# Softplus's logarithm as a degree-9 polynomial in the sigmoid, and one scan over all batches of a piece

## The reference

```python
# layer 0
a = xw_t + prev_h @ Wh
i, f, o = sigmoid(a[:, :H]), sigmoid(a[:, H:2*H]), sigmoid(a[:, 2*H:3*H])
g = tanh(a[:, 3*H:])
c = f * c + i * g ;  h = o * tanh(c)
x = x + hs
# layer 1
conv = conv_b + sum(x_pad[:, k:k+L, :] * conv_w[k, 0] for k in range(K))   # K = 8
proj = conv @ Wp + bp
B_t, C_t = softplus(proj[..., :N]), tanh(proj[..., N:])                    # N = 64
u = x @ Ws + bs
decay = 1 - softplus(dt_log) * softplus(A_log)
state = decay * state + softplus(dt_log) * B_t * u_t ;  y_t = C_t * state
x = x + y @ Wo + bo
```

## Time and profile before

| | before |
|---|---|
| median of 3 runs | 1922.39 us (1920.68 to 1922.65) |
| the profiled execution's own time | 1919.75 us |
| its span | 1917.8 us |
| granted TensorE clock, mean | 0.995 |
| busy: TensorE matmul, VectorE, ScalarE, GpSimd | 94%, 72%, 53%, 18% |

### The profile page before, as it was taken

The page is one execution under the profiler, slowest core; times in us unless marked ns, Lnnn a source line. Parts: engine busy times, 40 slices in busy tenths (PEclk is TensorE's granted clock), DMA queues, the critical chain, the costliest instruction groups (busy, mean ns, idle before and its releaser), DMA issues.

```text
span 1917.8 us, 123272 instructions
## 1 busy us (share of the span) xinstructions
PE 1810.3 (94%) x52690; PEld 1419.5 (74%) x52690; DVE 1388.6 (72%) x6911; ACT 1015.9 (53%) x4057; POOL 337.5 (18%) x1544
## 2 busy tenths in 40 slices
PE   5888999999999999999999999999999999999976
PEld 3666777777777777777777777777777777777865
DVE  8677667777677776777777677777777777867675
ACT  5555455555555555555555545555555555545442
POOL 1111111111111111111111111111111111111110
PEclk9999999999999999999999999999999999999998
DMA  6111111111111211111111111111111121211100
GB/s 236 53 42 38 48 54 37 51 55 44 53 51 39 63 43 54 44 50 55 48 57 40 54 54 42 59 45 51 53 53 45 46 56 40 74 38 50 46 15 24
DMA packets 112668, 100.81 MB, mean 53 GB/s; under 512 B 20353, under 2 KB 86453, under 8 KB 111094
## 3 DMA queue, kind: packets, MB, share of 16 engines
q1 hardware_dynamic: 111704, 90.79, 15.6%
q10 hardware_dynamic: 416, 2.13, 0.3%
HBM read 50.90 MB, written 41.94 MB: 48 GB/s over the span
## 4 chain that ended last, share of the span: by engine, by line
PE 78%; DVE 10%; ACT 5%; issue 3%; POOL 2%; DMA 1%; SPq 0%; ACTq 0%; POOLq 0%; DVEq 0%
PE recA L540 28%; PE recB L534 24%; PE pw L501 12%; PE pbc L585 10%; DVE tr L900 4%; ACT act L783 3%; POOL h L468 2%; DVE hz L931 2%; DVE pre L906 2%; DVE prod L914 1%; ACT tc L793 1%; PE pw L485 1%; PE po L605 1%; PE pu L558 1%; DMA wpk<-in_L_cond_Wh_dram 1%
## 5 line engine op out<-in xcount | busy, mean ns | idle before, releaser
L783 ACT ACTIVATE act<-pre 128x64 f32<-128x64 f32 x1024 | 262.7, 257 | 854.3 <-DVE pre L909 838.1
L540 PE MATMUL recA<-whi,hz 128*16 128x256 f16 x8176 | 516.0, 275 | 75.6 <-DVE hz L931 62.3
L534 PE MATMUL recB<-whi,hz 128*32 128x128 f16 x16352 | 577.6, 219 | 0.4 <-issue 0.4
L534 PE MATMUL recB<-wlo,hz 128*32 128x128 f16 x16352 | 577.6, 219 | 0.1
L540 PE MATMUL recA<-wlo,hz 128*16 128x256 f16 x8176 | 512.6, 273 | 0.0
L534 PEld LDWEIGHTS recB<-whi,hz 128*32 128x32 f16 x16352 | 438.0, 97 | 10.2 <-issue 0.6
L534 PEld LDWEIGHTS recB<-wlo,hz 128*32 128x32 f16 x16352 | 437.9, 97 | 2.6 <-issue 0.2
L540 PEld LDWEIGHTS recA<-whi,hz 128*16 128x16 f16 x8176 | 199.9, 88 | 303.5 <-DVE hz L931 281.6
L900 DVE STREAM_TRANSPOSE tr<-recA 128x256 f32<-128x256 f32 x512 | 230.0, 449 | 203.5 <-PE recA L540 201.6
L585 PE MATMUL pbc<-yt,wpk 128*128 128x256 f32 (+5 forms) x1120 | 329.6, 400 | 0.0
L468 POOL TENSOR_TENSOR h<-osc,tc 128x16 f32<-128x16 f32 x1024 | 226.3, 221 | 465.4 <-ACT tc L793 465.4
(11 more groups left out here) (157 smaller groups left out, 1989.8 us busy)
## 6 DMA issues: line engine op xcount, KB each, us to landing
xw_rows<-xs SPq DMA_DIRECT2D x128, 256.0 KB, 2.5
seed<-xw_rows SPq DMA_DIRECT2D x1008, 32.0 KB, 2.0
xn<-in_x_dram SPq DMA_DIRECT2D x32, 256.0 KB
out_dram<-ot SPq DMA_DIRECT2D x32, 256.0 KB, 3.0
seed<-in_L_cond_Wh_dram ACTq DMA_DIRECT2D x2, 1024.0 KB, 6.6
wpk<-in_L_cond_Wh_dram SPq DMA_DIRECT2D x2, 1024.0 KB, 12.2
wlo<-in_L_cond_Wx_dram SPq DMA_DIRECT2D x2, 1024.0 KB, 13.7
xs<-in_L_cond_Wx_dram SPq DMA_DIRECT2D x1, 1024.0 KB, 10.0
```

The lines of the kernel that those rows point to most:

```text
L534: ins = pe.matmul(rec[1][32 * j:32 * j + 32, 0:128], h[:, k, 2 * NB * (1 - c):2 * NB * (1 - c) + 32], w[:, k, 4 * (2 + c) + j, :], start=F ...
L540: ins = pe.matmul(rec[0][32 * j:32 * j + 2 * NB, 0:256].rearrange("p (c f) -> p c f", c=2), h[:, k, 2 * NB:4 * NB], w[:, k, :, :].rearrang ...
L783: act_eng.activation(act[q][:, 0:G, :].rearrange("p g n -> p (g n)"), pre[q][:, :, :, :].rearrange("p g c b -> p (g c b)"), ACT.Tanh, scal ...
```

## The change

It does two things. The logarithm becomes a polynomial in s itself: -log(1 - s) = s (c0 + c1 s + ... + c9 s^9), so `den`, `rcp`, `w` and `w2` are gone, `top` starts from the sigmoid, and there are 9 `term` instead of 7. And the 8 scans of a piece become one scan through all batches laid one behind another (in instructions of 128 columns: 2 for a wide piece, 1 for a narrow one). For that `drive` writes batch by batch (a stride of 32 or 16 elements against its inputs), the multiplier `dec` is 0 where a batch begins, and a new instruction `carry` adds the last state of the piece before, times decay, to the first element of each batch. `ys` turns the order back. `DVE_COST` gets the new names, so the plan is made anew.

```diff
-    SERIES = 7
+    LOG1M = (1.0, 0.5000016093254089, 0.3332335352897644, 0.25240495800971985, 0.17079266905784607,
+             0.3677962124347687, -0.6824740171432495, 2.1436290740966797, -2.655941963195801, 1.8215465545654297)
+    SERIES = len(LOG1M) - 1
...
-        def rcp_parts(key):
-            return 1 if key < 2 or span(key - 2)[3] <= COLS // 2 else 4
...
         def soft_order(key):
-            return ["abs", "sig", "pos"], ["den"] + ["rcp"] * rcp_parts(key) + ["w", "w2", "top"] + ["term"] * SERIES + ["sum"]
+            return ["abs", "sig", "pos"], ["top"] + ["term"] * SERIES + ["sum"]
...
-            return ["u"] + on_act + ["c"] + on_dve + ["drive"] + ["scan"] * NB + ["ys"]
+            return ["u"] + on_act + ["c"] + on_dve + ["drive", "carry"] + ["scan"] * (span(i)[3] // 128) + ["ys"]
...
-        DVE_COST = {"den": 0.33, "rcp": 0.46, "w": 0.34, "w2": 0.34, "top": 0.34, "term": 0.44, "sum": 0.44,
-                    "drive": 0.44, "scan": 0.2, "ys": 0.35}
+        DVE_COST = {"top": 0.34, "term": 0.44, "sum": 0.44,
+                    "drive": 0.44, "carry": 0.1, "scan": 0.4, "ys": 0.35}
...
+            def by_step(v):
+                return v.rearrange("p (t b) -> p t b", b=NB)
+
+            def by_batch(v):
+                return v.rearrange("p (b t) -> p t b", b=NB)
...
-                    dve.scalar_tensor_tensor(sp[:, 0:cols], sp[:, 0:cols], dtv[:, 0:1], us[:, 0:cols],
-                                             ALU.mult, ALU.mult).then_inc(s_drive, 1)
+                    dve.scalar_tensor_tensor(by_batch(acc[:, 0:cols]), by_step(sp[:, 0:cols]), dtv[:, 0:1],
+                                             by_step(us[:, 0:cols]), ALU.mult, ALU.mult).then_inc(s_drive, 1)
+                elif name == "carry":
+                    if i:
...
+                        first = acc[:, 0:cols:e - a]
+                        dve.scalar_tensor_tensor(first, st[:, (i - 1) % 2, ahead - 1:NB * ahead:ahead], decay[:, 0:1], first,
+                                                 ALU.mult, ALU.add).then_inc(s_drive, 1)
...
-                    ins = dve.tensor_tensor_scan(st[:, i % 2, 0:e - a, z], dec[:, 0:e - a], sp[:, z:cols:NB], init,
+                    ins = dve.tensor_tensor_scan(st[:, i % 2, some], dec[0 if e - a == TB else 1][:, :], acc[:, some], 0.0,
...
-                dve.tensor_tensor(ys[0:N, n % 2, NB * a:NB * e], ct[:, 0:cols],
-                                      st[:, i % 2, 0:e - a, :].rearrange("p t b -> p (t b)"),
+                dve.tensor_tensor(by_step(ys[0:N, n % 2, NB * a:NB * e]), by_step(ct[:, 0:cols]),
+                                      by_batch(st[:, i % 2, 0:cols]), ALU.mult).then_inc(s_ys, 1)
```

More of the change, by code:

```diff
@@ L84, in lstm_ssm_kernel @@
         sg = sb("sg", [N, COLS])
-        w2 = sb("w2", [N, COLS])
         acc = sb("acc", [N, COLS])
         ct = sb("ct", [N, COLS])
-        st = sb("st", [N, 2, TB, NB])
+        st = sb("st", [N, 2, COLS])
         ys = sb("ys", [N + 1, 2, COLS])
-        dec = sb("dec", [N, TB])
+        dec = [sb(f"dec{z}", [N, 128]) for z in range(2)]
         dtv = sb("dtv", [N, 2])
@@ L134, in lstm_ssm_kernel @@
         s_vecT, s_smT, s_ones, s_dec = (sem(n) for n in ("s_vecT", "s_smT", "s_ones", "s_dec"))
-        s_den, s_rcp, s_w, s_w2, s_ser, s_sp = (sem(n) for n in ("s_den", "s_rcp", "s_w", "s_w2", "s_ser", "s_sp"))
+        s_ser, s_sp = sem("s_ser"), sem("s_sp")
         s_dtv, s_drive, s_scan, s_ys = sem("s_dtv"), sem("s_drive"), sem("s_scan"), sem("s_ys")
@@ L966, in soft @@
                 S = lambda a: a[:, 0:cols]
-                if name == "den":
+                if name == "top":
                     dve.wait_ge(s_ssig, key + 1)
[L969 to L982, removed]
+                    dve.tensor_scalar(S(acc), S(sg), LOG1M[SERIES], None, ALU.mult).then_inc(s_ser, 1)
                 elif name == "term":
@@ L985, in soft @@
                     dve.wait_ge(s_ser, (SERIES + 1) * key + 1 + z)
-                    dve.scalar_tensor_tensor(S(acc), S(acc), 1.0 / (2 * i + 1), S(w2) if i else S(sg),
-                                             ALU.add, ALU.mult).then_inc(s_ser, 1)
+                    dve.scalar_tensor_tensor(S(acc), S(acc), LOG1M[i], S(sg), ALU.add, ALU.mult).then_inc(s_ser, 1)
                 elif name == "sum":
@@ L997, in post @@
                     dve.wait_ge(s_usb, i + 1)
-                    dve.scalar_tensor_tensor(sp[:, 0:cols], sp[:, 0:cols], dtv[:, 0:1], us[:, 0:cols],
-                                             ALU.mult, ALU.mult).then_inc(s_drive, 1)
+                    dve.scalar_tensor_tensor(by_batch(acc[:, 0:cols]), by_step(sp[:, 0:cols]), dtv[:, 0:1],
+                                             by_step(us[:, 0:cols]), ALU.mult, ALU.mult).then_inc(s_drive, 1)
+                elif name == "carry":
+                    if i:
+                        dve.wait_ge(s_drive, 2 * i)
+                        dve.wait_ge(s_scan, i)
+                        ahead = pieces[i - 1][2] - pieces[i - 1][1]
+                        first = acc[:, 0:cols:e - a]
+                        dve.scalar_tensor_tensor(first, st[:, (i - 1) % 2, ahead - 1:NB * ahead:ahead], decay[:, 0:1], first,
+                                                 ALU.mult, ALU.add).then_inc(s_drive, 1)
                 elif name == "scan":
                     if z == 0:
[L1002 to L1006, removed]
-                    ins = dve.tensor_tensor_scan(st[:, i % 2, 0:e - a, z], dec[:, 0:e - a], sp[:, z:cols:NB], init,
+                        dve.wait_ge(s_drive, 2 * i + 1)
+                    some = slice(128 * z, 128 * z + 128)
+                    ins = dve.tensor_tensor_scan(st[:, i % 2, some], dec[0 if e - a == TB else 1][:, :], acc[:, some], 0.0,
                                                  ALU.mult, ALU.add)
-                    if z == NB - 1:
+                    if z == cols // 128 - 1:
                         ins.then_inc(s_scan, 1)
@@ L1030, in param @@
                     dve.tensor_tensor(decay[:, :], dtv[:, 0:1], dtv[:, 1:2], ALU.mult).then_inc(s_dec, 1)
-                    dve.wait_ge(s_dec, 2)
+                    dve.wait_ge(s_dec, 5)
                     dve.tensor_scalar(decay[:, :], decay[:, :], -1.0, 1.0, ALU.mult, ALU.add).then_inc(s_dec, 1)
-                    dve.wait_ge(s_dec, 3)
-                    dve.tensor_scalar(dec[:, :], dec[:, :], decay[:, 0:1], None, ALU.mult).then_inc(s_dec, 1)
+                    dve.wait_ge(s_dec, 6)
+                    for z in range(2):
+                        dve.tensor_scalar(dec[z][:, :], dec[z][:, :], decay[:, 0:1], None, ALU.mult).then_inc(s_dec, 1)
                 else:
@@ L1058, in _ @@
             dve.memset(ys[N:N + 1, :, :], 1.0).then_inc(s_ones, 1)
-            dve.memset(dec[:, :], 1.0).then_inc(s_dec, 1)
+            for z in range(2):
+                dve.memset(dec[z][:, :], 1.0).then_inc(s_dec, 1)
+            dve.wait_ge(s_dec, 2)
+            for z in range(2):
+                dve.memset(dec[z][:, 0:128:TB >> z], 0.0).then_inc(s_dec, 1)
             for q in range(2):
```

4 lines of the change are left out of this document (1 added, 3 removed).

## The result

The changed kernel takes **1931.2 us** (median of 7 runs, 1929.52 to 1932.11), beside 1922.65 us for the kernel before (7 runs, 1920.68 to 1927.47): 8.55 us more, ratio 1.0047 with a 95% interval of 1.0038 to 1.0056. The forecast was 1928.8 us (1921.5 to 1933). The profiled execution took 1931.13 us with a span of 1929.2; the one before had a span of 1917.8, so the two traces differ by 11.4 us, 2.85 more than the medians.

What follows compares the result with a forecast made beforehand. Bound by the loop through VectorE, ScalarE and GpSimd, with about 0.1 us spare on TensorE in each slot. Terms 9.5 + 0.1 + 0.5 - 1.8 - 1.9 = +6.4 on 1922.39 gave 1928.8 us, range 1921.5 to 1933.

Steps and rivals of the forecast that it cites:

- What bounds the kernel: Each step: loop through VectorE, ScalarE and GpSimd at 3.56 us; side work free to 1.68 on TensorE, 0.86 on VectorE.
- The outputs' new slots: TensorE, third to thirteenth block: slots 12 to 16, 21 and 23 to 26 overfull, 0.86 us a block, +9.5 us.
- with the residual it is some 0.04 less: 0.04: Slots 21 and 24, a convolution, four residual transposes and three projections: each costs 0.04 us.
- The late part: Slots 416 to 492: TensorE's order +0.1 us; `carry` and both scans in one VectorE slot +0.5 us.
- Pieces 14 and 15: Steps 494 to 503 and 503 to 508, VectorE's slots less overfull: -0.7 and -1.1 us, together -1.8 (-1.2 to -2.6).
- I leave the cost in: Piece 15: the clock's fall to 1.2 GHz, costing up to 0.6 us before, is kept in the sum.
- The last piece: Behind the last step, VectorE's chain to `ys` takes 4.47 us instead of 6.41: -1.9 us (-1.4 to -2.3).
- The rival of the strides: `drive` and `ys` with strided operands each 0.27 us longer: +2.5 to +3, 1931.5 us; chance 0.12.
- The outputs are absorbed: Rival: late TensorE work in the outputs' slots is caught up next step, no 0.12 cost: 1919.3 us; chance 0.14.
- VectorE's busy time: VectorE, whole kernel: falls by an estimated 50 us, 15 wide pieces with 10 instructions fewer.

Runs made afterwards that it cites:

- experiment 2: Kernel before, only the projections' spread bent: slots 12 to 15 of each block from third to thirteenth hold five projections beside their convolution instead of four; 1924.4 us, ratio 1.0018.
- experiment 3: Kernel before, projections' spread bent further: of slots 12 to 15 of those blocks, three hold six projections and one five, instead of four; 1932.79 us, ratio 1.0054.
- experiment 8: On experiment 1: VectorE instructions a slot cut to 2 and 3 from 4 and 6 in pieces 14 and 15, their outputs moved up; 1913.68 us, ratio 0.996.
- experiment 1: Changed kernel with the outputs of steady pieces 0 to 10 put 8 slots later, where they stood before the change; 1919.14 us, ratio 0.9992.
- experiment 7: On experiment 1: `drive` and `ys` made contiguous, leaving out the reordering between steps and batches; 1918.76 us, ratio 0.9983.
- experiment 6: Kernel before with the single scan and `carry` but the old logarithm, `drive` and `ys` contiguous without reordering; 1923.2 us, ratio 1.0005.
- Experiment 5: Kernel before with only the scan's part (single scan, `carry`, strided `drive` and `ys`), old logarithm, run twice; 1924.71 us, ratio 1.0019, and 1925.41 us, ratio 1.0017.

## Why the prediction was right, step by step

*What bounds the kernel* (right). A step waits for its loop at 3.56 us; TensorE's slot is free up to 1.68 us and costs what it has above. Slots of 1.80 and 2.03 us in experiments 2 and 3 cost 0.11 and 0.34. VectorE's side is free up to 0.86: experiment 8 holds it there and the steps stay, and 0.89 costs some 0.05.

*The outputs' new slots* (right, +9.5 forecast, +10.8 in the slots named; 12.1 by the medians and 10.6 by the ratios between experiment 1 and the changed kernel, with 0.6 of the late part in it). The mis-sized part is the step "with the residual it is some 0.04 less: 0.04". It cost 0.09 in both slots, +1.1 in all: slot 21 at 1.78 has 0.21 more than the 1.57 of slot 237 with one projection fewer, so the four transposes take 0.44, about what a convolution or an output takes. Slot 8, 0.04 by itself, was not in the sum either; why it is longer wasn't found.

*The late part* (+0.1 and +0.5 forecast, +1.7 in the trace). The direction holds. Experiment 1's trace, in which the outputs of piece 11 leave this part, has +1.1 there, and experiment 7's, which differs from it by the strides alone, +0.7: so some 0.5 are these outputs and 0.5 the strides (`drive` at 0.66 instead of 0.48), and what is left is the forecast's 0.6.

*Pieces 14 and 15* (-0.7 and -1.1 forecast, -0.5 and -1.7 measured), together within the bounds. Part of this is luck of the profiled execution: "I leave the cost in", said of the fall of the clock, was wrong for it. The windows of the changed kernel, steps 505 and 506 (window, length, busy of PE, PEld, DVE, ACT, POOL, clock, DMA):

```profile
1885.17:1889.92 4.75, 2.48 (x98) 1.72 (x96) 3.84 (x20) 2.16 (x8) 0.65 (x3) 1.00 0.13 28
1889.92:1893.46 3.54, 1.24 (x57) 1.16 (x60) 2.90 (x15) 1.56 (x7) 0.65 (x3) 1.00 0.13 44
```

The granted clock is 1.00, that is 2.4 GHz, in both. Experiment 1 has the same instructions there, and in its profiled execution the same two steps read:

```profile
1872.56:1877.33 4.77, 2.84 (x78) 2.03 (x80) 3.85 (x20) 2.16 (x8) 0.65 (x3) 0.82 0.14 30
1877.33:1881.84 4.51, 2.92 (x84) 2.17 (x76) 2.94 (x15) 1.56 (x7) 0.67 (x3) 0.50 0.11 36
```

The second step is at 0.50, or 1.2 GHz, and takes 4.51 us instead of 3.54; from step 505 to step 508 it is 1.4 us more. So the fall cost 1.35 where the forecast had up to 0.6; without it the sum of 2.4 above 17.8 is what was measured (2.35). Of the ten traces that have the long slots of piece 15, nine show a fall between steps 505 and 508, the kernel before with 0.75 among them, and only the changed kernel's does not. So the cost did belong in the sum, as 1.35: with the fall on both sides piece 15 gives -0.4 (21.50 against 21.86), not -1.1. In experiment 8, where no slot is long, the window from step 503 to 508 reads 1.00:

```profile
1859.26:1877.34 18.08, 12.31 (x525) 10.32 (x516) 14.43 (x73) 10.32 (x42) 3.23 (x15) 1.00 0.07 19
```

*The last piece* (-1.9 forecast; the chain to `ys` was forecast at 4.47 and took 4.60, so -1.8; the whole stretch after step 511 gave -2.1, and the rest of that stands ahead of the chain, in 0.4 us for which the forecast had no term). From start to start, `drive` with its stride took 0.46 where 0.38 stood and `carry` 0.26 where 0.20 stood; the terms came out as forecast. **The scan was over-sized: 0.47 forecast, 0.41 measured**, 0.45 from its start to that of `ys`. The slope of 2.06 ns an element was right; the base was not. The two rows it was drawn through, 270 and 237 ns, are of scans that start from a value in memory. The kernel before has one group that starts from 0, the first piece's, in the view of the earlier trace rows, though not among its rows:

```profile
L1007 DVE TENSOR_TENSOR_SCAN st<-dec,sp 64x32 f32<-64x32 f32 x8 | 1.4, 210 | 0.0
```

210 ns at 32 elements and 408 at 128 give 2.06 ns again, and the new scan starts from 0: it is 60 ns cheaper. The base of this group would have given 0.41.

*The rival of the strides* was half true. They cost 0.18 us each, not 0.27, and it isn't they that made the kernel slower: experiment 1 has them all and is even with the kernel before, and taking them out is worth 0.4 to 2.3 us (experiments 7 and 6). The Trainium skill (SBUF — State Buffer, the note on cachelines under Door 1) has accesses that cross into a new 16-byte line pay a penalty; the trace agrees in kind, and puts it at 0.7 ns an element of a float32 instruction on VectorE. But the scans of before, with a stride of 8 elements on both sides, give 210 ns and 2.06 ns an element; carried on to 128 elements that is 408 ns, which is what the new ones take without a stride. So a stride of 8 adds nothing to the scan that shows. *The outputs are absorbed* fell with slot 111 at 3.68.

*VectorE's busy time* fell by 37 us where 50 was estimated, 5.4 of the difference by the strides. Nothing in the time hangs on it.

In all, the terms missed the same way and not against each other: the blocks and the late part came out dearer by 1.3 and 1.1 us, which is most of why the medians are 8.55 apart and not 6.4. The sign and the main term are no luck.

## What to carry to other kernels

When a change shortens a list that a planner works off, look first at what is timed from the end of that list: here shorter work on VectorE pulled the outputs on TensorE forward by 8 slots, onto the convolutions, and 37 us less work became 9 us more time. Measure how much room a slot has on each engine (one slot that is full and one that is not), and price every slot by what stands above it; a sum of averages says nothing, since TensorE has as many matmuls after as before. And work saved beside a chain is worth something only when the plan is changed to use it: in the steady part the saved instructions gained nothing, and the 6 us between experiments 1 and 8 came from the way pieces 14 and 15 were laid out.

## What was not expected of the hardware

- A stride of 32 elements on one side of a 64x256 float32 instruction on VectorE adds 0.18 us (477 to 659 and 417 to 596 ns). On the scan a stride of 8 adds nothing that shows.
- A scan that starts from a value in memory is 60 ns longer than one that starts from 0 (270 and 210 ns at 64x32).
- The clock fell in one execution and not in another of the same instructions, after the same long VectorE slot: 0.97 us on one step. Behind the last step it fell some 2.5 us earlier in one execution of a kernel than in another: 1.8 us.
- Steps that are 0.1 to 0.5 us longer stand scattered through every trace, 16 to 25 of the 352. Most of them belong to the program and not to the execution. Experiment 5 ran one kernel twice, and 20 of the 21 long steps of each trace are the same steps. VectorE's steps 376 and 377 in the first and in the second:

```profile
1398.45 0.45 DVE L900 STREAM_TRANSPOSE tr<-recA 128x256 f32<-128x256 f32 x1 [0.18 <-PE recA L540]
1402.39 0.45 DVE L900 STREAM_TRANSPOSE tr<-recA 128x256 f32<-128x256 f32 x1 [0.58 <-PE recA L540]
...
1398.62 0.45 DVE L900 STREAM_TRANSPOSE tr<-recA 128x256 f32<-128x256 f32 x1 [0.18 <-PE recA L540]
1402.56 0.45 DVE L900 STREAM_TRANSPOSE tr<-recA 128x256 f32<-128x256 f32 x1 [0.58 <-PE recA L540]
```

3.94 us in both, where the kernel before has 3.56. The kernel before and experiment 2, with the same instructions on VectorE, share 17 of their long steps; the kernel before and experiment 5 share 2. A single step of 0.4 to 1.0 us, such as the changed kernel's step 218, comes on top in some executions and not in others. What the fixed ones wait for no run showed. A single pair of traces can't tell less than about 2 us.

**Open:** the scan alone came out 3 us above the kernel before, twice, and its slots account for under 1, its scattered steps, which lie elsewhere than before, for 0.8 to 0.9 more (5.4 and 5.5 us in all against 4.6). Without the strides it is 2 us less, of which slot 20 accounts for 0.7 and piece 14 for 0.4. What the rest waits for no run showed.
